# Mixture-of-experts rows added into the token array in DRAM, tile by tile, by GpSimd's indirect DMAs, in place of a combining pass at the end

## The reference, cut to what matters

```
def _L1_ffn_ref(x, uzman_embeddings, W1, b1, W2, b2, onbellek_durumu):
    tokens = x.reshape(-1, D)                                  # 4096 x 256
    global_idx, weights = _route(tokens, ...)                  # two experts and two weights per token
    h = jnp.einsum('nd,edh->enh', tokens, W1) + b1[:, None, :] # hidden width 1024
    h = jax.nn.gelu(h, approximate=False)
    out_all = jnp.einsum('enh,ehd->end', h, W2) + b2[:, None, :]
    out_sel = out_all[global_idx, jnp.arange(N)[:, None]]
    return jnp.sum(weights[..., None] * out_sel, axis=1)
...
h = _layernorm(x, axis=-1) * (1 + cb) + sb
x = x + gb * _L1_ffn_ref(h, ...)                               # gb: one row of 256 gates per sequence
```

## Time and profile before

| | |
|---|---|
| median of 3 executions | 3454.5 us (3439.14 to 3456.36) |
| the profiled execution: its time | 3460.88 us |
| its span, from first to last instruction | 3459.0 us |
| mean granted TensorE clock over the span | 0.824 of full |
| busy shares of the span | PE 77%, DVE 51%, ACT 34%, POOL 16% |

### The profile page before, as it was taken

The page is one execution under the profiler, slowest core; times in us unless marked ns, Lnnn a source line. Parts: engine busy times, 40 slices in busy tenths (PEclk is TensorE's granted clock), DMA queues, the critical chain, the costliest instruction groups (busy, mean ns, idle before and its releaser), DMA issues.

```text
span 3459.0 us, 77272 instructions
## 1 busy us (share of the span) xinstructions
PE 2669.2 (77%) x33792; PEld 1969.6 (57%) x33792; DVE 1775.3 (51%) x3867; ACT 1167.3 (34%) x2276; POOL 565.9 (16%) x613
## 2 busy tenths in 40 slices
PE   3468777968896987788788968887696659999980
PEld 3244466446545654564565456555554558888870
DVE  4644766494658547664956585466438410100004
ACT  0322454254335324542453253335125312222210
POOL 0004200600250052006001500430000000000006
PEclk8668886988798778778886978797698779999995
DMA  2122201401120122013011201220110055556645
GB/s 80 31 63 55 50 18 43 95 8 45 50 62 8 45 68 50 2 57 94 12 45 44 67 8 45 62 50 2 57 49 2 10 189 192 192 192 192 193 161 167
DMA packets 229984, 246.99 MB, mean 71 GB/s; under 512 B 147408, under 2 KB 187216, under 8 KB 227344
## 3 DMA queue, kind: packets, MB, share of 16 engines
q1 hardware_dynamic: 223504, 225.27, 22.0%
q0 software_dynamic: 6144, 16.79, 1.5%
HBM read 195.88 MB, written 46.14 MB: 70 GB/s over the span
## 4 chain that ended last, share of the span: by engine, by line
PE 64%; DVE 17%; ACT 9%; issue 5%; POOL 2%; DMA 1%; SPq 1%; POOLq 0%; DVEq 0%; ACTq 0%
PE banks L1927 19%; PE banks L2449 8%; PE banks L2468 8%; PE banks L2240 4%; PE banks L2159 3%; PE banks L2260 2%; PE banks L2265 2%; PE banks L1937 2%; POOL arena L1867 2%; PE banks L2194 2%; DVE hT L1512 2%; PE banks L2029 1%; PE banks L2001 1%; PE banks L2070 1%; ACT arena L893 1%
## 5 line engine op out<-in xcount | busy, mean ns | idle before, releaser
L1927 PE MATMUL banks<-hT,ring 128*128 128x512 f32 x640 | 300.4, 627 | 7.8 <-DVE arena L1364 7.8
L1844 POOL DMA_INDIRECT h_d<-h_tok,pos_now x64 | 65.0, 1015 | 1453.3 <-DVE pos_now L1683 1291.4
L2240 PE MATMUL banks<-arena 32*32 32x64 f32 (+2 forms) x6144 | 191.5, 303 | 135.4 <-DVE arena L1520 64.5
L1069 ACT ACTIVATE arena<-banks,arena 128x256 f32<-128x256 f32 x312 | 131.0, 471 | 457.0 <-PE banks L2449 457.0
L2449 PE MATMUL banks<-arena 128*128 128x256 f32 x1248 | 276.3, 380 | 0.0
L2468 PE MATMUL banks<-arena 128*128 128x256 f32 x1248 | 275.7, 379 | 0.0
L2240 PE MATMUL banks<-arena,xn 32*32 32x64 f32 (+2 forms) x6144 | 178.8, 299 | 123.1 <-DVE xn L1520 65.6
L2240 PEld LDWEIGHTS banks<-arena 32*32 32x32 f32 (+2 forms) x6144 | 170.7, 181 | 174.3 <-issue 78.8
L2449 PEld LDWEIGHTS banks<-arena 128*128 128x128 f32 x1248 | 237.5, 190 | 32.7 <-issue 0.4
L2468 PEld LDWEIGHTS banks<-arena 128*128 128x128 f32 x1248 | 234.2, 190 | 30.3
L2240 PEld LDWEIGHTS banks<-arena,xn 32*32 32x32 f32 (+2 forms) x6144 | 165.4, 179 | 140.4 <-DVE xn L1520 75.6
(11 more groups left out here) (349 smaller groups left out, 4763.9 us busy)
## 6 DMA issues: line engine op xcount, KB each, us to landing
arena<-in_w_ring SPq DMA_DIRECT2D x78, 1024.0 KB, 5.0
ring<-in_w_ring SPq DMA_DIRECT2D x104, 512.0 KB, 4.3
arena<-h_d SPq DMA_DIRECT2D x39, 256.0 KB, 5.4
y_d<-arena SPq DMA_DIRECT2D x39, 256.0 KB, 5.9
n_d<-NA SPq DMA_DIRECT2D x8, 1024.0 KB, 3.8
arena<-n_d SPq DMA_DIRECT2D x16, 512.0 KB, 5.8
u_d<-arena SPq DMA_DIRECT2D x8, 1024.0 KB, 3.8
NA<-u_d SPq DMA_DIRECT2D x32, 256.0 KB, 5.9
```

The source lines that it names most:

```text
L1069: ins_ = act.activation(hid1[:, i % 2, t], bank[pair][:, half * T1:(half + 1) * T1], ACT.Gelu, bias=b1[:, i % 2, t:t + 1])
L1927: i_ = mm(dst, w[:, k, cols_], rhs(src, k), start=(k == 0), stop=(k == n - 1))
L2240: i_ = mm(bank[4 * hg + h][keys, b * width:(b + 1) * width], K2[rows_, r, b, keys], q, start=(r == 0), stop=(r == 1), skip_group_check=True)
```

## The change

The combining pass and `y_d` go. `x_d` becomes a plain array of tokens (4096 rows and 256 rows that belong to nobody), and each expert tile is added into it.

- For each destination row in `h_d` there is now a row of five numbers in `info_d`: the token's number, and its share in the place of its sequence (zero in the other three). Each segment ends with 8 more indirect DMAs that scatter these rows of 20 bytes, and GpSimd waits for them too.
- In the last segment GpSimd counts `started` up ahead of its scatters, not after them, so that the plan can begin while they run. SP loads `w1` of tile 0, waits for `h_out` and only then stores the zeros. Further stores fill the unused rows of `info_d` (`nobody`) and the spare rows of `x_d`.
- For each tile DVE builds `factor` (gates times shares, 8 operations of 128x256), and then takes three operations in place of one: add `b2`, multiply by the factor, add the fetched rows `acc_rows`.
- GpSimd runs through the tiles: two indirect fetches from `x_d` (128 rows each), a wait for `y_ok`, two indirect scatters of the sums back to `x_d`, and a wait until they have landed (`y_out`) ahead of the next tile's fetch, since a token can be in both tiles.
- At the end SP copies `x_d` to the output, DRAM to DRAM, in 4 DMAs of 1 MB.

```diff
@@ SP, after the segments
-            for e in range(E1):
-                r = sp.value_load(pad_i[0:1, e:e + 1], ...)
-                sp.dma_start(h_d[bass.ds(r, T1)]..., zeros).then_inc(*up16(zero_out))
-            sp.dma_start(h_d[E1 * REGION:]..., zeros).then_inc(*up16(zero_out))
...
-            for i in range(2):
-                load_w1(i)
+            def load_info(i):
+                r = sp.value_load(plan_i[0:1, 1, i:i + 1], min_val=0, max_val=E1 * REGION)
+                if i >= INFOS:
+                    sp.wait_ge(y_out.handle, 32 * (i - INFOS + 1))
+                sp.dma_start(info_rows[:, i % INFOS], info_d[bass.ds(r, T1)]...).then_inc(*up16(info_in[i % INFOS]))
+
+            load_w1(0)
             sp.wait_ge(h_out.handle, h_out.base(NSEG))
+            for e in range(E1):
+                ...
+                sp.dma_start(h_d[bass.ds(r, T1)]..., zeros).then_inc(*up16(zero_out))
+            sp.dma_start(h_d[E1 * REGION:]..., zeros).then_inc(*up16(zero_out))
             sp.wait_ge(zero_out.handle, 16 * (E1 + 1))
             for i in range(2):
                 load_rows(i)
+            load_w2(0)
+            load_w1(1)
+            load_w2(1)
+            sp.wait_ge(nobody_ok.handle, 2)
+            sp.wait_ge(info_out.handle, info_out.base(NSEG))
+            for e in range(E1):
+                ...
+                sp.dma_start(info_d[bass.ds(r, T1)]..., nobody).then_inc(*up16(pad_out))
+            sp.dma_start(info_d[E1 * REGION:]..., nobody).then_inc(*up16(pad_out))
+            sp.dma_start(x_d[B * L:]..., zeros).then_inc(*up16(pad_out))
+            sp.wait_ge(pad_out.handle, 16 * (E1 + 2))
             for i in range(2):
-                load_w2(i)
+                load_info(i)
             for i in range(TILES1):
                 if i + 2 < TILES1:
                     sp.wait_ge(turned.handle, i + 1)
                     load_rows(i + 2)
+                    load_info(i + 2)
                     sp.wait_ge(hid1_ok.handle, 4 * (i + 1))
                     load_w1(i + 2)
                 if i:
                     sp.wait_ge(y_ok.handle, i)
                     if i + 1 < TILES1:
                         load_w2(i + 1)
-                    store_rows(i - 1)
...
+            sp.wait_ge(y_out.handle, 32 * TILES1)
+            for b in range(B):
+                sp.dma_start(out[b]..., x_d[b * L:(b + 1) * L]...).then_inc(*up16(made_out))
@@ DVE, one tile
+                dve.wait_ge(info_in[i % INFOS].handle, 16 * (i // INFOS + 1))
+                factor, made = factors[:, i % 2], y_rows[:, i % 2]
+                for b in range(B):
+                    for j in range(2):
+                        weight = info_rows[:, i % INFOS, j, 1 + b:2 + b]
+                        if b == 0:
+                            ins_ = dve.tensor_scalar(factor[:, j], gates[:, 1, 1, b], weight, None, ALU.mult)
+                        else:
+                            ins_ = dve.scalar_tensor_tensor(factor[:, j], gates[:, 1, 1, b], weight, factor[:, j],
+                                                            ALU.mult, ALU.add)
+                    plan_step(ins_)
                 dve.wait_ge(down_mm.handle, i + 1)
                 if i >= 2:
-                    dve.wait_ge(y_out[i % 2].handle, 16 * (i // 2))
-                dve.tensor_tensor(y_rows[:, i % 2], bank[4 + i % 2]..., b2[...], ALU.add).then_inc(*up(y_ok))
-            (the combining loop over 8 segments)
+                    dve.wait_ge(y_out.handle, 32 * (i - 1))
+                plan_step(dve.tensor_tensor(made, bank[4 + i % 2]..., b2[...], ALU.add))
+                plan_step(dve.tensor_tensor(made, made, factor, ALU.mult))
+                dve.wait_ge(acc_back.handle, 32 * (i + 1))
+                dve.tensor_tensor(made, made, acc_rows[:, i % 2], ALU.add).then_inc(*up(y_ok))
@@ POOL, after the segments
+            for i in range(TILES1):
+                pool.wait_ge(info_in[i % INFOS].handle, 16 * (i // INFOS + 1))
+                if i:
+                    pool.wait_ge(y_out.handle, 32 * i)
+                ...
+                for j in range(2):
+                    pool.indirect_dma_start(out=acc_rows[:, i % 2, j], ..., in_=x_d, in_offset=spots[j])
+                pool.wait_ge(y_ok.handle, i + 1)
+                for j in range(2):
+                    pool.indirect_dma_start(out=x_d, out_offset=spots[j], in_=y_rows[:, i % 2, j], ...)
```

More of the change, by code:

```diff
@@ L156, in build @@
         next_row = sb("next_row", [P, E1])
-        where = sb("where", [P, NSEG, 2, B])
-        y_at = sb("y_at", [P, NSEG, 2, B], U32)
-        share = sb("share", [P, NSEG, 2, B])
+        info = sb("info", [P, 2, B, INFO])
         pos_now = sb("pos_now", [P, 2 * B], U32)
@@ L362, in build @@
         h_out = signal("h_out", rest=16 * 2 * B)
+        info_out = signal("info_out", rest=16 * 2 * B)
+        id_ok = signal("id_ok", rest=1)
+        info_ok = signal("info_ok", rest=1)
         n_out = signal("n_out", nxt=16)
@@ L481, in build @@
         rows_in = [signal(f"rows_in{i}") for i in range(2)]
-        y_out = [signal(f"y_out{i}") for i in range(2)]
+        y_out = signal("y_out")
+        info_in = [signal(f"info_in{i}") for i in range(INFOS)]
+        acc_back = signal("acc_back")
         turned = signal("turned")
@@ L488, in build @@
         y_ok = signal("y_ok")
-        y_back = [signal(f"y_back{i}") for i in range(3)]
-        x_back = [signal(f"x_back{i}") for i in range(3)]
-        mixed_ok = signal("mixed_ok")
-        mixed_out = [signal(f"mixed_out{i}") for i in range(3)]
+        made_out = signal("made_out")
         last = {}
@@ L1683, in turn @@
                     dve.tensor_copy(pos_now[:, :], pos.rearrange("p k b -> p (k b)")).then_inc(*up(pos_ok, me))
-                    this = slice(seg, seg + 1)
-                    step(dve.tensor_copy(where[:, this].rearrange("p s k b -> p (s k b)"), pos.rearrange("p k b -> p (k b)")))
                     dve.wait_ge(*at(rt_exp, 1))
@@ L1689, in turn @@
                     step(dve.tensor_tensor(rs[:, 14], rs[:, 11], rs[:, 13], ALU.mult))
[L1690 to L1691 removed]
+                    if seg:
+                        dve.wait_ge(info_out.handle, info_out.base(seg))
+                    dve.tensor_copy(info.rearrange("p k b w -> p k (b w)")[:, :, 1:2 + (B - 1) * (INFO + 1):INFO + 1],
+                                    rs[:, 13:15]).then_inc(*up(info_ok, me))
                     step(dve.tensor_tensor(next_row[:, :], next_row[:, :], ranks[:, B * E1:], ALU.add))
@@ L1745, in _ @@
             dve.tensor_copy(pad_i[0:1, :], next_row[0:1, :]).then_inc(*up(plan_ok))
-            plan_step(dve.tensor_tensor(shift, end, tiles, ALU.subtract))
-            plan_step(dve.scalar_tensor_tensor(shift, shift, float(T1), region[:, :], ALU.mult, ALU.subtract))
-            plan_step(dve.tensor_tensor(jump[:, 1:], shift[:, 1:], shift[:, 0:E1 - 1], ALU.subtract))
-            spots = where[:, :, :, :].rearrange("p s k b -> p (s k b)")
-            moved, part = plan[:, 3, 0:NSEG * 2 * B], plan[:, 4, 0:NSEG * 2 * B]
-            plan_step(dve.tensor_copy(moved, spots))
-            for e in range(1, E1):
-                plan_step(dve.tensor_scalar(part, spots, float(REGION * e), jump[:, e:e + 1], ALU.is_ge, ALU.mult))
-                plan_step(dve.tensor_tensor(moved, moved, part, ALU.add))
-            dve.tensor_copy(y_at[:, :, :, :].rearrange("p s k b -> p (s k b)"), moved).then_inc(*up(spots_ok))
             def columns(i):
@@ L1845, in turn @@
                                 .then_inc(h_out.handle, 16)
+                    pool.wait_ge(*at(id_ok, 1))
+                    pool.wait_ge(*at(info_ok, 1))
+                    for k in range(2):
+                        for b in range(B):
+                            spot = bass.IndirectOffsetOnAxis(ap=pos_now[:, k * B + b:k * B + b + 1], axis=0)
+                            pool.indirect_dma_start(out=info_d, out_offset=spot, in_=info[:, k, b, :], in_offset=None)\
+                                .then_inc(info_out.handle, 16)
                     pool.wait_ge(h_out.handle, h_out.base(seg + 1))
+                    pool.wait_ge(info_out.handle, info_out.base(seg + 1))
                 else:
```

109 lines of the change are left out of this document (47 added, 62 removed).

## The result

The changed kernel takes 3503.8 us (median of 4, 3490.57 to 3505.55), the kernel before beside it 3455.0 (median of 4): ratio 1.0143, 95% interval 1.0113 to 1.0173. It is **1.4% slower**; the prediction said 2.1% faster, with 6 chances in 100 for slower. The profiled execution has a span of 3500.7 us, 41.7 more than before.

The account below looks back on a forecast made before the run. PE was taken to bound the tile loop, with a 98.1 us combining pass behind it. Removing that, +8.3 last chain, +24.6 copy, -6 seam, 0 loop and segments gave -71.2: median 3383 us, range 3366 to 3428.

Parts of the forecast that it names:

- The segments: Segment ends: eight more indirect DMAs, 10.2 us plus landing, fit in GpSimd's 24.3 us of idle time, costing 0 us.
- a loop that stays PE's: 0 us: Tile loop: landings of about 4.5 us give a 12.7 us chain, under PE's 14.26 us period, so no loss.
- the first rival: Tile loop: the fetch-and-scatter chain bounds it yet the change wins; period 14.9 to 15.5 us, loss 25 to 47; 27 in 100.
- the prediction's own sum: Tile loop: the chain between two tiles' y_ok is 3.7 us of wake-ups, issues and addition, plus two landings.
- the estimate of 10 us by the rule: Tile loop: with queues served round-robin by packet, GpSimd's blocks wait little and the chain is near 10 us.
- The seam: Between last segment and tile loop: earlier plan and loads bring the first down 6 us earlier, between 2 and 8.
- The tail: After the last product: chain adds 8.3 us, the DRAM-to-DRAM copy 24.6 us, the combining pass's 98.1 us go.
- DVE starves GpSimd: Tile loop: DVE operations stretch GpSimd's issues to 1.75 us, chain 15.9 us, time 3444 us; 4 in 100.
- Slower: Tile loop: chain beyond 16.1 us, landings over 6.2 us each, makes the change a loss; 6 in 100.

Follow-up runs that it names:

- Experiments 1 to 5: Indirect scatters added to the kernel before (3538.1 to 3541.3 us), moved later there (3431.8) or in the changed kernel (3419.4); plain transfers (3453.4, 3467.2) or multiplications (3469.5) added.
- Experiment 7: Changed kernel with w1 and w2 loaded in full for tiles 0 and 1 only, 8 columns for later tiles: 3454.6 us, period 14.12 us.
- experiment 1: Kernel before with eight more indirect scatters per segment end, of 20 bytes or 1 KB a row: 3539.1 and 3541.3 us.
- Experiment 10: Padding stores moved from SP's queue to GpSimd, zeros ahead of the h_out wait: 3491.9 us in the changed kernel, 3366.0 with late scatters and new load order too.
- Experiment 3: Changed kernel with all 16 scatters of each of segments 0 to 6 moved behind the next segment's substitution: 3419.4 us, ratio 0.9902 to the kernel before.
- experiment 2: Kernel before with the eight scatters of segments 0 to 6 moved behind the next segment's substitution: 3431.8 us, ratio 0.9921.

## Why the prediction was wrong

**The step that failed first** is "The segments": "GpSimd idles 24.3 us there before it can go on the earlier trace rows, waiting for a transfer that none of this feeds: 0 us, with 11 us of cover." Measured are +63.7 us, more than the whole net loss of 41.7. The cover was there (26.6 us of idle time were left), and it didn't help. I asked whether GpSimd had time, and it had. I didn't ask what its issuing does to PE beside it. Experiments 1 to 5 show it: the number of indirect scatters that GpSimd issues beside the run of 32x32 products sets the loss, whatever they carry. The rows of before would have told it: the same run takes 1.90 us for 128 products at 274.64 and comes in pieces at 585.39, and the pieces end 1 us behind GpSimd's last issue.

**The second** is "a loop that stays PE's: 0 us". The mechanism was there as the first rival, with its price: at landings of 5.9 a period of 15.5 and +47 us. Measured are a period of 15.4 and +50.5 us. With the medians, 6.6 and 5.3, the prediction's own sum gives 3.7 + 11.9 = 15.6. What was mis-sized are the landings, the scatter's above all: I took 4.5 for both, between 2.6 and 5.6, while the earlier trace rows and the 5.9 in the earlier trace rows were the rows nearest to a transfer beside 1 MB bursts. Experiment 7 shows that these bursts are the cause. The way to PE was wrong too: not `y_ok` but DVE's copy behind the addition, and rows behind `y_ok` in SP's queue; I had given both a tile of slack. The Trainium skill's rule in "DMA: Bandwidth & Descriptors" (section on queues, rings and completion order), round-robin by packet, had let me keep a short landing possible; a chain of 15.4 is close to the 15 that the earlier trace rows taken as they stand gave, and the estimate of 10 us by the rule does not hold here.

**The seam**, predicted -6 at the start of the first `down`, measured 58.2 - 55.4 = +2.8 there, had its mechanism right (tile 2's rows behind ten stores) and two terms too small. From the last padding store to tile 2's rows it took 2882.05 - 2871.88 = 10.2 us, not 5.4: the store landed in 7.1 us, not 2.1. And the zeros for `h_d` began 2842.71 - 2827.54 = 15.2 us behind the first scatter, where I had `h_out` in at 11.6: GpSimd's second scatter went out 1.9 us late, the last one's landing took 1.0 us more, and 0.7 is SP's reading of a register. The early plan beside it isn't why the second was late, as the kernel of experiment 1, without an early plan, has the same 1.9 us; the cause stays open. The slow clock behind PE's wait was no term at all. Experiment 10 returns 9.8 us.

**The tail** was right in sign, and better than predicted: last tile's end to the end 20.0 us, predicted 29.5 from the same mark. The copy is the term: 15.2 us, not 24.6. Read and write did not share one rate of 378 GB/s.

**The rivals.** "DVE starves GpSimd" is refuted: the 156 issues in the loop take 0.95 to 1.13 us, and the 35 of them beside the factor's `tensor_scalar` operations 1.01 on average, the others 0.98. The 1.75 us of the earlier trace rows stood beside two TENSOR_TENSOR operations of 128x1024 (L1788, L1790), not beside `tensor_scalar`. "Slower" was right by its sign, not by its mechanism: the period stayed under its 16.1 us, and without the segments the change would have won 78.9 - 50.5 - 6.4 = 22 us. Experiment 3 wins 36 beside the kernel before: these 22, and part of what the scatters had cost the kernel before itself. So 6 in 100 for slower was too little, as no rival had a place outside the loop. One reading was off and changes nothing: in the earlier trace rows PE is at 9 in five slices of the tiles and at 8 in the sixth.

**Left open** is how an indirect scatter holds up TensorE's small products. It isn't bytes, rows, plain transfers of the same engine, or its arithmetic. Whether it is the issue or what follows it isn't told either: full pace comes back 1 to 3 us behind the end of the last issue. The pauses end on "issue", with no semaphore, and the first 33 to 44 products of a run still go at full pace beside the issues. A supply of instructions that runs dry would look like this, as 15 ns products use it up fastest, but no run here shows it. Indirect fetches beside such a run weren't tried.

## What to carry to other kernels

An engine with idle time can still cost another engine time by what it issues, here indirect DMAs: look for where a run of many small instructions on one engine is in one piece in a stretch without that traffic and in pieces with it, and move the traffic beside few, large instructions. A chain through DRAM in a loop is priced with the landing beside the loop's own bursts, not with a quiet one; then start the bursts so that they are over at the next landing. Look too at what stands behind the chain's wait in each engine's program: here a copy that PE needed. Stores that only fill unused places don't belong ahead of a load that an engine waits for.

## What the runs showed of the hardware

- GpSimd's indirect scatters hold up a run of 192 of TensorE's 32x32 products: 3.7 us alone (experiment 2, a short wait for DVE included), 9.3 with 8 of them, of which 5 fall into the run, 20.0 with 16, of which 12 do. That is 1.1 to 1.4 us for each, where an issue with its pause lasts 1.27. Beside plain GpSimd transfers 134 products take 2.89 us.
- An indirect scatter of 16 rows of 20 bytes costs 0.84 us to issue, one of 128 rows of 1 KB 0.97.
- A scatter of 128 rows of 1 KB from the second issue on: 2.5 us with quiet queues, 7.1 beside a 1 MB weight load (median 6.6).
- A copy of 4.19 MB from DRAM to DRAM in 4 DMAs: 15.2 us with issue and landing, 335 GB/s while it moves.
- TensorE's granted clock fell from 1.00 to 0.50 in an idle time of 9.7 us; 32 products of 128x256 behind it took 9.1 us, where they take 7.07 at 1.00.
